# Sharing the layer norms of four decoder tails between ScalarE and VectorE

## What is computed

```python
def _layernorm(x, axis=-1, eps=1e-05):
    m = jnp.mean(x, axis=axis, keepdims=True)
    v = jnp.var(x, axis=axis, keepdims=True)
    return (x - m) / jnp.sqrt(v + eps)
...
    x = _layernorm(x + _L0_attn_ref(x, ...))             # selective scan (1024 channels, 16 states) and an FFN
    x = _layernorm(x + _L0_xattn_ref(ctx_1024, x, ...))  # second scan (512 channels), gated by silu(x)
    x = _layernorm(x + _L0_ffn_ref(x, ...))              # two of eight experts per token, and a shared one
    x = _layernorm(x + _L1_attn_ref(x, ...))             # attention of 4-token segments with a memory
    x = _layernorm(x + _L1_xattn_ref(x, ctx_1024, ...))  # x times softmax(q k) over 512 features
    x = _layernorm(x + _L1_ffn_ref(x, ...))              # top 8 of 64 router scores, expert biases
```

## Time and profile before

| | |
|---|---|
| three timed runs | 3062.4, 3063.85, 3065.66 us; median 3063.85 |
| the profiled execution | 3062.09 us, its span 3060.3 us |
| busy over the span | TensorE 2543.3, VectorE 2422.9, ScalarE 1190.6, GpSimd 1053.4 us |
| mean granted TensorE clock | 0.902 |

### The profile page before, as it was taken

How to read it: one execution, slowest core, us unless ns; L and a number is a source line. 1 busy time by engine, 2 the same in 40 slices (tenths; PEclk the granted TensorE clock), 3 DMA queues, 4 the chain that set the end, 5 groups by cost and what they waited for, 6 DMA issues and landing times.

```text
span 3060.3 us, 21508 instructions
## 1 busy us (share of the span) xinstructions
PE 2543.3 (83%) x6908; PEld 1222.8 (40%) x6908; DVE 2422.9 (79%) x1788; ACT 1190.6 (39%) x1952; POOL 1053.4 (34%) x299
## 2 busy tenths in 40 slices
PE   4777989888979887789798785898787859999997
PEld 1234434333434443344344443343444424455554
DVE  5997898988989988899899998898999985121122
ACT  4334446444253452443433533433445432021222
POOL 1333343344434445424434454244443442001000
PEclk6886999998989998789889997899799879999999
DMA  4124426332212674022116650221155512216930
GB/s 134 33 79 162 139 105 199 103 105 100 65 38 88 221 239 142 26 101 64 42 67 206 222 175 20 95 83 48 66 183 184 183 44 69 76 45 208 296 110 14
DMA packets 160391, 350.14 MB, mean 114 GB/s; under 512 B 30680, under 2 KB 48088, under 8 KB 155608
## 3 DMA queue, kind: packets, MB, share of 16 engines
q1 hardware_dynamic: 134680, 271.89, 28.4%
q10 hardware_dynamic: 20480, 60.10, 5.2%
q0 software_dynamic: 5120, 16.78, 1.7%
HBM read 304.55 MB, written 61.73 MB: 120 GB/s over the span
## 4 chain that ended last, share of the span: by engine, by line
PE 40%; DVE 33%; issue 14%; ACT 5%; POOL 4%; DMA 3%; ACTq 0%; DVEq 0%; SPq 0%; POOLq 0%
DVE hb L1634 14%; PE ps L969 7%; PE ps L976 6%; DVE hb L1642 5%; PE ps L777 4%; DVE hb L1547 4%; PE ps L824 3%; PE ps L942 3%; PE ps L831 3%; POOL ya L1907 2%; DMA ring<-in_w_edn 2%; PE ps L1127 2%; PE ps L1012 2%; PE ps L899 1%; DVE sm L1496 1%
## 5 line engine op out<-in xcount | busy, mean ns | idle before, releaser
L1907 POOL TENSOR_TENSOR ya<-ya,hb 128x2048 f32<-128x2048 f32 x188 | 857.0, 4559 | 1318.9 <-DVE hb L1634 1007.2
L1634 DVE TENSOR_TENSOR_SCAN hb<-da,hb 128x2048 f32<-128x2048 f32 x192 | 856.2, 4459 | 1.5 <-ACT da L1175 0.2
L1175 ACT ACTIVATE da<-dl,pk 128x511 f32<-128x511 f32 x768 | 489.7, 711 | 423.1 <-DVE hb L1634 409.2
L1547 DVE TENSOR_TENSOR hb<-du,ps 128x2048 f32<-128x2048 f32 x192 | 435.8, 2270 | 33.4 <-POOL ya L1907 27.4
L1642 DVE TENSOR_TENSOR hb<-hb,ps 128x2048 f32<-128x2048 f32 x192 | 437.4, 2278 | 3.7 <-PE ps L916 2.9
L824 PE MATMUL ps<-V,ring 128*128 128x512 f32 x512 | 237.9, 616 | 22.0 <-DVE V L1575 9.1
L777 PE MATMUL ps<-ring,hid 128*128 128x512 f32 x544 | 245.7, 608 | 3.7 <-DVE hid L1679 3.7
L993 PE MATMUL ps<-ring,hid 128*128 128x352 f32 x480 | 197.0, 494 | 21.8 <-ACT hid L1404 15.6
L997 PE MATMUL ps<-ring,hid 128*128 128x352 f32 x480 | 192.0, 483 | 11.8 <-ACT X L1421 11.7
L1012 PE MATMUL ps<-ring,X 128*128 128x512 f32 x360 | 181.1, 639 | 12.9 <-DMA ring<-in_w_edn 12.1
L969 PE MATMUL ps<-T,ring 128*128 128x512 f32 x352 | 166.1, 616 | 17.4 <-DVE T L1667 17.4
(11 more groups left out here) (283 smaller groups left out, 3434.2 us busy)
## 6 DMA issues: line engine op xcount, KB each, us to landing
ring<-egu SPq DMA_DIRECT2D x240, 352.0 KB, 3.8
ring<-in_w_edn SPq DMA_DIRECT2D x72, 512.0 KB, 5.2
ring<-in_w_fgu SPq DMA_DIRECT2D x44, 512.0 KB, 3.6
hid<-xrows SPq DMA_DIRECT2D x60, 256.0 KB, 4.2
yrows<-X ACTq DMA_DIRECT2D x60, 256.0 KB, 4.6
ring<-wc SPq DMA_DIRECT2D x24, 512.0 KB, 4.1
ring<-in_w_egu SPq DMA_DIRECT2D x24, 512.0 KB, 3.5
ring<-in_w_edn SPq DMA_DIRECT2D x60, 192.0 KB, 4.1
```

Source lines behind the costliest of these rows:

```text
L1175: i = act.activation(dav(n % 2)[:, k, 1:], dl[:, k, 1:], ACT.Exp, scale=Aneg[:, (4 * (u % 3 - 1) if u % 3 else UC) + k, m:m + 1])
L1547: dve.tensor_tensor(hbv(m % NHB), du[:, :, :], wide(ps[:, 5, :], 4), ALU.mult).then_inc(s["dbu"], 1)
L1634: dve.tensor_tensor_scan(hb[:, h, :], da[:, b % 2, :], hb[:, h, :], 0.0, ALU.mult, ALU.add)\
L1907: pool.tensor_tensor(sums, ya[:, :, :], hbv(m % NHB), ALU.add).then_inc(s["acc"], 1)
```

## The change

ScalarE keeps tiles 0 and 2 of each norm, and makes only their two shifts. VectorE gets two tasks. `ln_d` waits for the root and writes tiles 1 and 3 by one `tensor_scalar` each, (tile + negated mean) x root. `ln_x` waits for the transposes and copies chunks 1 and 3 to `X`; ScalarE copies 0 and 2. Since the tiles now come ready out of order, their readers wait for all four: `v_in`, `gate` and `seg_r` for each tile of `nat`, the transposes of norm 2, `s_in` for all four copies instead of two, `x_in` likewise. `KEEP` loses four matmuls in the wait ahead of each of the five norms' readers and two behind three of the transpositions, 26 in all. `SHARE` holds all four sequences. That makes 18 new instructions per tail on VectorE, ten of `ln_d` and eight of `ln_x`, and takes 28 from ScalarE: ten shifts, ten tiles and eight copies.

```diff
+SHARE = range(SEQS)
-KEEP = [(("t_sq", 0), ("ffn_mm", 0), 6), (("res_t", 0), ("v_in", 0), 12), (("v_in", 0), ("gate", 0), 3),
+KEEP = [(("t_sq", 0), ("ffn_mm", 0), 6), (("res_t", 0), ("v_in", 0), 8), (("v_in", 0), ("gate", 0), 3),
...
             chain(30, ("ln", b, n), [("dve", us + 0.3), ("act", 5.6)], at)
+            if b in SHARE:
+                put(30, ("ln_d", b, n), "dve", 1.4, (("ln", b, n), "act", -2.9))
             if n:
-                chain(30, ("ln_t", b, n), [("pe", 3.6), ("act", 2.4)], (("ln", b, n), "act", -0.6 if n == 2 else 0))
+                chain(30, ("ln_t", b, n), [("pe", 3.6), ("act", 2.4)], (("ln", b, n), "act", -0.6 if n == 2 else 0),
+                      (("ln_d", b, n), "dve") if b in SHARE else None)
+                if b in SHARE:
+                    put(30, ("ln_x", b, n), "dve", 1.3, (("ln_t", b, n), "pe"))
...
-                            pe.wait_ge(*of("nrm", b, 4 * (n - 1) + (e + 1 if n == 2 else TT)))
+                            pe.wait_ge(*of("nrm", b, 4 * (n - 1) + (e + 1 if n == 2 and b not in SHARE else TT)))
...
-                            pe.wait_ge(*of("v", b, e + 1))
+                            pe.wait_ge(*of("v", b, TT if b in SHARE else e + 1))
...
-                            pe.wait_ge(*of("xe", b, 6))
+                            pe.wait_ge(*of("xe", b, 8 if b in SHARE else 6))
...
-                            pe.wait_ge(*of("xe", b, 8 + e + 1))
+                            pe.wait_ge(*of("xe", b, 12 if b in SHARE else 8 + e + 1))
...
-                        for e in range(TT):
+                        mine = range(0, TT, 2) if b in SHARE else range(TT)
+                        for e in mine:
                             i = act.activation(shift[:, e:e + 1], mv[:, e, 0:1], ACT.Copy, scale=r4[:, e:e + 1])
...
-                        for k in range(KC):
+                        for k in range(0, KC, 2) if b in SHARE else range(KC):
                             act.activation(X[:, k, :], ps[:, k, :], ACT.Copy).then_inc(s["xe"], 1)
...
-                            act.wait_ge(*of("v", b, e + 1))
+                            act.wait_ge(*of("v", b, TT if b in SHARE else e + 1))
...
+                    elif t == "ln_d":
+                        dve.wait_ge(*of("rstd", b, (2, 3, 4, 6, 7)[n]))
+                        for e in range(1, TT, 2):
+                            dve.tensor_scalar(nat[:, e, :], (nat if n == 2 else ps)[:, e, :], mv[:, e, 0:1], r4[:, e:e + 1],
+                                              ALU.add, ALU.mult).then_inc(s["nrm" if n else "v"], 1)
+                    elif t == "ln_x":
+                        dve.wait_ge(*of("nat", b, n + 1))
+                        for k in range(1, KC, 2):
+                            dve.tensor_copy(X[:, k, :], ps[:, k, :]).then_inc(s["xe"], 1)
```

More of the change, by code:

```diff
@@ L42 @@
 HOP, SLACK, LOAD = 0.15, 0.4, 4.5
-KEEP = [(("t_sq", 0), ("ffn_mm", 0), 6), (("res_t", 0), ("v_in", 0), 12), (("v_in", 0), ("gate", 0), 3),
-        (("gate", 0), ("ln_t", 1), 15), (("ln_t", 1), ("route_a", 0), 3), (("exp_down", 5), ("ln_t", 2), 16),
-        (("ln_t", 2), ("s_in", 0), 6), (("s_in", 1), ("seg_e", 0), 4), (("seg_e", 0), ("seg_t", 0), 2),
-        (("seg_t", 0), ("ln_t", 3), 8), (("xmix", 3), ("ln_t", 4), 12), (("ln_t", 4), ("bias_a", 0), 3),
+SHARE = range(SEQS)
+KEEP = [(("t_sq", 0), ("ffn_mm", 0), 6), (("res_t", 0), ("v_in", 0), 8), (("v_in", 0), ("gate", 0), 3),
+        (("gate", 0), ("ln_t", 1), 11), (("ln_t", 1), ("route_a", 0), 1), (("exp_down", 5), ("ln_t", 2), 12),
+        (("ln_t", 2), ("s_in", 0), 4), (("s_in", 1), ("seg_e", 0), 4), (("seg_e", 0), ("seg_t", 0), 2),
+        (("seg_t", 0), ("ln_t", 3), 4), (("xmix", 3), ("ln_t", 4), 8), (("ln_t", 4), ("bias_a", 0), 1),
         (("bias_a", 0), ("bias_b", 0), 9), (("bias_b", 0), ("bias_c", 0), 1)]
@@ L296, in plan @@
         norm(0, (("res_t", b, 0), "pe"), 3.5)
-        put(30, ("v_in", b, 0), "pe", 2.0, (("ln", b, 0), "act"))
-        chain(30, ("gate", b, 0), [("act", 2.4), ("dve", 5.6), ("pe", 3.6)], (("ln", b, 0), "act"), (("sb", NST * (3 * b + 1) - 1, 0), "pool"))
+        put(30, ("v_in", b, 0), "pe", 2.0, (("ln", b, 0), "act"), (("ln_d", b, 0), "dve") if b in SHARE else None)
+        chain(30, ("gate", b, 0), [("act", 2.4), ("dve", 5.6), ("pe", 3.6)], (("ln", b, 0), "act"),
+              (("ln_d", b, 0), "dve") if b in SHARE else None, (("sb", NST * (3 * b + 1) - 1, 0), "pool"))
         nodes[("gate", b, 0), "pe"][2].append((("v_in", b, 0), "pe", 0))
@@ L1461, in _ @@
                         for e in range(TT):
-                            act.wait_ge(*of("nrm", b, 4 + e + 1))
+                            act.wait_ge(*of("nrm", b, 4 + (TT if b in SHARE else e + 1)))
                             i = act.activation(hid[:, e, :], nat[:, e, :], ACT.Square, accum_out=rq[:, e:e + 1])
```

## The result

The kernel with the change takes 3102.73 us (median of four runs, 3099.93 to 3105.75) against 3064.76 us for the kernel before (four runs), ratio 1.0123, 95% interval 1.0107 to 1.0138: 38 us slower, where 13 were forecast. The profiled execution has a span of 3098.6 us.

A forecast was written before the change was run, and what follows sets the result against it. VectorE was taken to bound the kernel until 2546 us, a chain of latencies in tail 3 after that. 34.0 - 12.3 - 8.1 = +13.6 us on the profiled 3062.1 gave 3077 us by the timed runs, range 3058 to 3097.

The forecast's parts named there:

- Added work: Before the last scan ends, 14 `ln_d` and 11 `ln_x` pairs add 34.0 us of VectorE's time.
- port rival: Norm 2's SBUF-form `ln_d` stalls beside a GpSimd sum, 3 to 4 us per tail: 3087 us; chance 0.08.
- What waits take back: Before the last scan, new VectorE work fills existing waits for other engines, giving back 12.3 us.
- norm 0 of tail 0: `ln_d` fills VectorE's wait for the gate's first tanh, leaving 9.2 us idle against 9.7: 0.5 back.
- The ends of units 5 and 8: `ln_x` ahead of `fin`, norm 4 behind `dt_c`: 4 us back at unit 5, 2 at unit 8.
- The row ahead of the `hb` waits: Feature attention's last row moves ahead of the `hb` buffer wait in tails 0 and 1: 2.4 us back.
- The slip rival: In the tails, `ln_d` and `ln_x` wait for turns behind scans, making TensorE late: +32 us, 3095; chance 0.2.
- has been made with the later times: Argument against late tails: VectorE's waits for TensorE are small in sum, and the planned order already allows for later times.
- The sign that would show it: Waits for TensorE appearing in tails 1 and 2 that were not there would prove the prediction wrong.
- Tail 3: After the last scan, norms 0, 1, 2 and 4 get shorter and norm 3 loses 0.3: -8.1 us in sum.
- I take no new drop: In tail 3 TensorE's granted clock, 0.98 and nearly all at 2.4 GHz, was assumed not to fall further.

The follow-up runs named there:

- old_order: Whole change, but `ln_d` and `ln_x` put into the order of the kernel before, at the first place found ready; 3110.64 us, 1.0146.
- tiles_only: Kernel before with only `ln_d` shared, in tails 0 to 2; ScalarE still makes all copies; 3106.2 us, 1.0144.
- round_trip: Tails 0 to 2 planned and waiting as when shared, but ScalarE does all tiles and copies; VectorE's `ln_d`, `ln_x` do one unused column; 3102.77 us, 1.0129.
- order_only: Kernel before with the orders planned for sharing tails 0 to 2, but none of the change in the engines' programs; 3090.86 us, 1.0088.
- keep_back: Change in tail 3 alone, with useless matmuls given back ahead of `v_in` (8 to 12) and norm 2's transposes (12 to 18); 3055.58 us, 0.9973.
- last_only: Changed kernel with `SHARE` holding sequence 3 only, so the change is in tail 3 alone, with its shorter `KEEP`; 3060.12 us, 0.9982.
- order_tail0: Kernel before with only tail 0 planned with the two new tasks, nothing of the change in the programs; 3072.76 us, 1.0038.
- steps_first: Whole change, with norm 3's transposes of tails 0 and 1 behind the next unit's `dt_mm` on TensorE; 3114.37 us, 1.0169.

## Why the prediction was wrong

**Added work: right.** +34.0 us against +30.9 measured, of which the new instructions themselves are 31.9. `ln_d` and `ln_x` by source line (min/median/max ns), against the earlier trace rows:

```profile
L1725 DVE TENSOR_SCALAR T<-ps,mv,sm x32: 784/802/811, 892.0 to 3061.3; 128x512 f32<-128x512 f32 x32
L1725 DVE TENSOR_SCALAR T<-T,mv,sm x8: 539/542/547, 1248.9 to 3001.9; 128x512 f32<-128x512 f32 x8
```

```profile
L1730 DVE COPY X<-ps x32: 659/680/692, 918.2 to 3065.2; 128x512 f32<-128x512 f32 x32
```

None stretches, so the port rival is out in this kernel. That the 18 of these PSUM reads that lie beside a sum of GpSimd (6 tiles, 12 copies) never did agrees with the rule that the prediction takes from the Trainium skill ("SBUF — State Buffer", section "SBUF: two separate sides"); norm 2's SBUF form never lay beside one here, and so shows nothing. In `old_order` and `tiles_only` it did, and took 4.72 us at the three places where the sum was already running. The prediction was saved there by where the planner happened to put `ln_d`: that the sum is over by then holds for this order and not for the other.

**What waits take back, -12.3 us: this step failed.** It was +16.5, a miss of 28.8 us. Item by item: norm 0 of tail 0 gave 0.3 us back (forecast 0.5), the waits 8.63 and 0.77 instead of 8.64 and 1.10 of the earlier trace rows; tails 1 and 2 cost 6.7 and 6.4 us instead of giving back 1.7 each. The ends of units 5 and 8 cost 6.0 and 5.1 (11.1 to 17.1, 9.5 to 14.6) instead of giving back 4 and 2. The row ahead of the `hb` waits gave nothing of 2.4: 27.4 us before, 27.4 after. These items are +23.9 together. At the two ends of units 4.8 us of that came back in the waits beside them (for `mix`, 2.2 us before and 0.4 after, above all), and 2.6 in many small ones. The error behind all of them is one: I kept the other engines' arrival times fixed and asked only what VectorE's new work would fill. The waits named as cover are waits for TensorE and ScalarE, and the change made those later.

**The slip rival was the true case**, given a chance of 0.2 and a time of 3095. Its mechanism is shown: the loss is there without the work (`round_trip`, +1.29%), and about two thirds of that with the new order alone (`order_only`, +0.88%). Its price was too small by some 8 us. It was worked out as one late step per tail, 2 x 9 us beside the taken-back 12.3; in fact next to nothing was taken back, and the lateness is paid at two places, at the end of the tail and at norm 0 of the next, since the next sequence's FFN starts later too. The argument against it, that the order "has been made with the later times", was worthless: the order itself costs 27 us. The sign that would show it, waits for TensorE in tails 1 and 2 that were not there, came as written.

**Tail 3, -8.1 us: right in kind, off by 2.3.** Measured -5.8. Norms 1 and 4 each gained 2.5 us from the root to the next matmul (7.88 to 5.40), as forecast; norm 4, against the earlier trace rows:

```profile
3060.56 0.48 ACT L1437 ACTIVATE sm<-mv,sm 128x1 f32<-128x1 f32 x2
3060.56 1.53 DVE L1725 TENSOR_SCALAR T<-ps,mv,sm 128x512 f32<-128x512 f32 x2 [0.60 <-ACT sm L1176]
3061.07 1.45 ACT L1441 ACTIVATE T<-ps,sm 128x512 f32<-128x512 f32 x2
...
3064.59 1.09 ACT L1446 ACTIVATE X<-ps 128x512 f32<-128x512 f32 x2 [2.06 <-PE ps L1042]
3064.59 1.29 DVE L1730 COPY X<-ps 128x512 f32<-128x512 f32 x2 [2.49 <-PE ps L1042]
```

Norm 3 lost 0.26 us against 0.3, for the reason given: `ln_d` behind the row maximum, against the earlier trace rows (the prediction's text has the two groups swapped: it calls norm 3's rows and norm 2's):

```profile
3029.09 0.69 DVE L1796 TENSOR_REDUCE sm<-ps 128x1 f32<-128x512 f32 x1 [1.71 <-PE ps L1104]
3029.70 1.52 DVE L1725 TENSOR_SCALAR T<-ps,mv,sm 128x512 f32<-128x512 f32 x2
...
3034.63 3.70 PE L1061 MATMUL ps<-T,pk 128*128 128x512 f32 x8 [0.94 <-DVE X L1730]
```

Norm 2 gained 0.9 instead of 1.8 and norm 0 0.1 instead of 1.6. "I take no new drop" of the clock was the step that failed: the two drops shown above, undone by `keep_back`, whose last scan to end is 522.1 us against 525.0 in `last_only`.

**Open.** In what proportion the two places share the order's 27 us is not settled: `order_tail0` holds one tail and reached 7.8 us in the profile, 11 in the median. Nor is it known what TensorE's clock adds: from the first to the last scan the granted clock is 0.891 before, 0.880 in the changed kernel and 0.877 in `order_only`, and no run holds the clock fixed. At the end of unit 5 it is some 3.6 us, in the 32 us ahead of norm 0 of tail 1 nothing. Nor was it tried whether an order exists in which the three tails share their norms without a loss.

## What to carry to other kernels

Before work is moved to a saturated engine with an order of its own, count what waits for it there. Two microseconds handed to it in the middle of another engine's chain cost a turn behind a 4.5 us scan, and here the turns, with the order planned round them, cost three times what the work did (+1.29% without the work, +0.43% for work without turns). A wait may be counted as cover only if its releaser is not made later by the same change. Where the moving engine is idle, as in tail 3, the same split gains, and filler matmuls sized for the old wait have to be measured against the new one. And a wait that vanishes under a change of order is no gain until the whole kernel is timed: `steps_first` removed the wait of 12.66 us that it aimed at, and was the slowest of all.

## What the hardware showed beside that

TensorE's granted clock fell to 1.2 GHz behind 2.30 and 3.21 us without work, which made a 3.70 us stage 5.34 us, and stayed full behind 0.58 and 0.62 us at the same two places. The length of the wait isn't all: behind 2.22 us at norm 3 it stayed full in two kernels and fell in `keep_back`. So the useless matmuls have a right number and not only a cost: four and six more of them took 2.9 us off the end of the profiled execution (525.0 to 522.1 from the last scan on). In the timed runs that is 0.9982 against 0.9973, with intervals that overlap.

`tensor_scalar` on 128x512 with input and output in SBUF took 0.54 us alone and 4.72 us when a sum of GpSimd was running as it started (`old_order`); with its input in PSUM it took 0.80 us in both cases. How many of VectorE's SBUF instructions meet such a sum changes with the order, so VectorE's busy time from the first to the last scan was 7.9 us less in `order_tail0` than in the kernel before, with the same work.
